# Two cross attentions of a decoder: projections in pairs, maxima earlier

## The reference

```python
# first block: 16 heads of 8
qc = _heads(x @ Wcq + bcq)
kc = _heads(cross_input @ Wck + bck)
vc = _heads(cross_input @ Wcv + bcv)
attc = jnp.einsum('bhqd,bhkd->bhqk', qc, kc) * scale
y = y + jnp.einsum('bhqk,bhkd->bhqd', jax.nn.softmax(attc, axis=-1), vc)
...
# second block, _mha of x over the normed context: 16 heads of 32
q = jnp.einsum('bsc,hcd->bhsd', xn, wq)
k = jnp.einsum('btc,hcd->bhtd', yn, wk)
v = jnp.einsum('btc,hcd->bhtd', yn, wv)
a = jax.nn.softmax(jnp.einsum('bhsd,bhtd->bhst', q, k) * D ** (-0.5), axis=-1)
o = jnp.einsum('bhst,bhtd->bhsd', a, v)
```

## Time and profile before

| what | us |
|---|---|
| median of 3 runs | 2286.98 |
| lowest, highest | 2262.93, 2294.28 |
| the profiled execution | 2294.59 |
| its span, first to last instruction | 2292.4 |
| busy in it: TensorE | 1837.0 (80%) |
| VectorE, ScalarE, GpSimd | 1177.9, 969.5, 524.5 |
| first cross attention, first to last shift matmul | 323.1 |
| last cross attention, first query product to its output projection | 602 (1478.2 to 2080.3) |

### The profile page before, as it was taken

How to read it: one execution, slowest core, us unless ns; L and a number is a source line. 1 busy time by engine, 2 the same in 40 slices (tenths; PEclk the granted TensorE clock), 3 DMA queues, 4 the chain that set the end, 5 groups by cost and what they waited for, 6 DMA issues and landing times. The chain is left out here.

```text
span 2292.4 us, 42946 instructions
## 1 busy us (share of the span) xinstructions
PE 1837.0 (80%) x16607; PEld 1007.5 (44%) x16607; DVE 1177.9 (51%) x2374; ACT 969.5 (42%) x1576; POOL 524.5 (23%) x392
## 2 busy tenths in 40 slices
PE   2774584999998339989899498579999999997598
PEld 1452361232233316654466265324445445454365
DVE  2664487777773335448642466434555555541322
ACT  1442262777776222211354244214554554553133
POOL 2112312000000000006544000024445445442000
PEclk8896696788887659999999779759999999998699
DMA  8414322211110221000000000021121121100010
GB/s 221 126 52 127 88 67 47 44 43 43 32 29 1 97 56 42 28 14 1 1 1 1 1 2 16 5 54 37 41 51 38 41 51 36 42 23 1 19 37 28
DMA packets 111896, 96.47 MB, mean 42 GB/s; under 512 B 21696, under 2 KB 97128, under 8 KB 111208
## 3 DMA queue, kind: packets, MB, share of 16 engines
q1 hardware_dynamic: 111720, 94.04, 15.7%
HBM read 51.30 MB, written 19.86 MB: 31 GB/s over the span
## 5 line engine op out<-in xcount | busy, mean ns | idle before, releaser
L2102 DVE TENSOR_REDUCE ta_mxp<-ps 128x1 f32<-128x401 f32 x512 | 267.2, 570 | 275.9 <-PE ps L2021 275.8
L1154 DVE TENSOR_REDUCE ac_mxp<-ps 128x2 f32<-128x802 f32 x256 | 244.7, 991 | 91.6 <-PE ps L1070 90.2
L2125 ACT ACTIVATE ta_prob<-ps 128x2048 f32<-128x2048 f32 (+1 forms) x112 | 196.5, 1755 | 146.9 <-PE ps L2057 146.9
L1183 ACT ACTIVATE cT<-ps 128x512 f32<-128x512 f32 (+1 forms) x416 | 225.7, 595 | 62.9 <-PE ps L1095 54.9
L1109 PE MATMUL ps<-cT 128*32 128x256 f32 (+1 forms) x1664 | 157.5, 456 | 0.5 <-ACT cT L1183 0.5
L2021 PE MATMUL ps<-ta_kb,ta_qb 96*128 96x401 bf16 x512 | 138.6, 355 | 16.4 <-DMA ta_kb<-ta_kh 12.2
L2053 PE MATMUL ps<-qxf,ta_k 32*128 32x256 f32 (+1 forms) x1664 | 133.6, 405 | 12.8 <-ACT ta_shiftT L2143 9.2
L2565 PE MATMUL ps<-xT,e_wi 128*128 128x512 f32 x256 | 116.1, 613 | 15.0 <-DMA e_wd<-in_e_down 10.2
L1070 PE MATMUL ps<-ac_kb,ac_qz 50*128 50x401 bf16 x512 | 100.7, 401 | 25.2 <-DMA ac_qb<-qc 18.5
L2575 PEld LDWEIGHTS ps<-e_wd,e_hid 128*128 128x128 f32 x1024 | 116.9, 192 | 7.6 <-issue 7.6
L2188 POOL TENSOR_TENSOR yT<-ta_prob 128x1024 f32<-128x1024 f32 x40 | 94.0, 2350 | 110.1 <-ACT ta_prob L2125 93.6
(11 more groups left out here) (323 smaller groups left out, 3507.0 us busy)
## 6 DMA issues: line engine op xcount, KB each, us to landing
ta_kb<-ta_kh SPq DMA_DIRECT2D x128, 100.1 KB
ac_kb<-kc SPq DMA_DIRECT2D x192, 50.0 KB
ta_kb<-ta_kl SPq DMA_DIRECT2D x64, 100.1 KB
v<-p_vt SPq DMA_DIRECT2D x16, 256.0 KB, 3.2
a_vs<-v SPq DMA_DIRECT2D x32, 128.0 KB, 2.7
e_wi<-in_e_in SPq DMA_DIRECT2D x8, 512.0 KB, 3.5
e_wd<-in_e_down SPq DMA_DIRECT2D x16, 256.0 KB, 3.6
kc<-c_part SPq DMA_DIRECT2D x12, 300.0 KB, 3.0
```

The costliest lines, as they stand in the source:

```text
L1154: v.tensor_reduce(mxp[:, qt * G + 2 * gg:qt * G + 2 * gg + 2, c:c + 1], k.ps[:, i % 2 * 2:i % 2 * 2 + 2, 0:401], AX.X, ALU.max).then_inc(s ...
L1183: a.activation(prob[0:rows, n % 3, h, :], k.ps[0:rows, bank(("part", n, h)), :], ACT.Exp, scale=scale).then_inc(exp_done.s, 1)
L2102: v.tensor_reduce(mxp[:, qt * G + g, c:c + 1], k.ps[:, turns.bank(slot), 0:401], AX.X, ALU.max).then_inc(scores_read.s, 1)
L2125: a.activation(prob[0:rows, n % 3, :, 0:w], k.ps[0:rows, 2:6, 0:w], ACT.Exp, scale=scale).then_inc(exp_done.s, 1)
```

## The change

In `stage_long` the count of plain products runs six key tiles ahead instead of three (EARLY), with a cap for the first tiles, and none but the first group's are issued ahead of the first shift. In the last cross attention groups s and s + 1 (s even) now belong to two batches that lie on the two halves of the partitions; their key chunks, and their value tiles, are issued next to each other (in even groups the keys of the next two, in odd ones the values of the next two). `Turns` gives a step three lists: three maxima; the other maxima, between values and row sums; projections after the row sums. `weigh` is split into `values` and `ones`. `stage_queries` is gone: the stage makes the queries itself after three key pairs, keeps their bf16 halves for a while in two buffers of the exponents, stores them to memory on SP, and loads a group's from there. Key and value buffers go from three to four and from two to three. The first negation is a scalar_tensor_tensor (−2 m + m) instead of a tensor_scalar.

```diff
-    NS, G, KT, NBUF, SLOTS, EARLY = BH // 4, 4, KT_CTX, 4, 16, 3
+    NS, G, KT, NBUF, SLOTS, EARLY = BH // 4, 4, KT_CTX, 4, 16, 6
...
-        return min(NS * SLOTS, SLOTS + (n + EARLY) * SLOTS // KT)
+        return min(NS * SLOTS, SLOTS + min((n + EARLY) * SLOTS // KT, 3 * (n + 1) // 2 + 1))
...
-                for i in range(SLOTS, issued(-1) if issued(-1) > SLOTS else SLOTS):
-                    plain_scores(i)
                 shift_rows(0)
-                done = max(SLOTS, issued(-1))
+                done = SLOTS
...
-                if 0 <= s + 2 < groups and p < 4:
-                    late.append(("key", s + 2, p))
-                if 0 <= s + 1 < groups and 2 <= p < 6:
-                    late.append(("value", s + 1, p - 2))
-                if 0 <= s + 1 < groups and p == STEPS - 1:
-                    late.append(("shift", s + 1, 0))
+                if s % 2 == 0 and s + 2 < groups and p < 4:
+                    late += [("key", s + 2, p), ("key", s + 3, p)]
+                if s == -2 and p >= 3:
+                    late += [("value", 0, p - 3), ("value", 1, p - 3)]
+                if s % 2 == 1 and 0 < s + 1 < groups and p < 4:
+                    late += [("value", s + 1, p), ("value", s + 2, p)]
                 m = [("max", s + 1, n) for n in range(*MAX_AT[p])] if 0 <= s + 1 < groups else []
                 early, m = m[0:3], m[3:]
-                mixed = []
-                for a, b in itertools.zip_longest(late, m):
-                    mixed += [x for x in (a, b) if x is not None]
-                for when, some in ((0, early), (1, mixed)):
+                if 0 <= s + 1 < groups and p == STEPS - 1:
+                    m.append(("shift", s + 1, 0))
+                for when, some in ((0, early), (1, m), (2, late)):
...
-MAX_AT = ((0, 6), (6, 12), (12, 17), (17, 22), (22, 27), (27, 32), (32, 32))
+MAX_AT = ((0, 5), (5, 10), (10, 15), (15, 20), (20, 26), (26, 32), (32, 32))
...
-def stage_queries(nc, k, srcT, w, full, high, low):
...
-def stage_cross(nc, k, name, scale, cT, wk, wv, q, qh, ql, both, out):
+def stage_cross(nc, k, name, scale, cT, wk, wv, srcT, wq, q, qh, ql, both, out):
...
+    def batch(s):
+        return s // 8 + 2 * (s % 2)
+
+    def part(s):
+        return s // 2 % 4
+
     def half(s):
-        return slice(64 * (s // 8), 64 * (s // 8) + 64)
+        return slice(64 * (s % 2), 64 * (s % 2) + 64)
 
     def at_batch(s):
-        return (s // 4) % 2 * W
+        return s // 8 * W
...
-        k32 = sb("k32", [P, 3, T_CTX])
+        k32 = sb("k32", [P, 4, T_CTX])
...
-        vs = sb("vs", [P, 2, KT_CTX, P])
+        vs = sb("vs", [P, 3, KT_CTX, P])
...
+        high_q, low_q = (prob[:, n, :, :].rearrange("p g c -> p (g c)").bitcast(BF16).rearrange("p (j c) -> p j c", j=4)
+                         for n in range(2))
+        units = [(j, c) for j in range(4) for c in range(2)]
...
+                    if kind in ("key", "value") and s % 2 == 1:
+                        return
                     free(slot)
                     bank = k.ps[:, turns.bank(slot), :]
-                    j = s % 4
+                    if kind in ("key", "value"):
+                        free((kind, s + 1, n))
+                        banks = (bank, k.ps[:, turns.bank((kind, s + 1, n)), :])
+                        j = part(s)
...
-                        pe.matmul(bank[:, 0:w], wk[half(s), j * P:(j + 1) * P],
-                                  cT[half(s), at_batch(s) + t0:at_batch(s) + t0 + w],
-                                  start=True, stop=True).then_inc(made.s, 1)
+                        for r in (s, s + 1):
+                            pe.matmul(banks[r % 2][:, 0:w], wk[half(r), j * P:(j + 1) * P],
+                                      cT[half(r), at_batch(r) + t0:at_batch(r) + t0 + w],
+                                      start=True, stop=True).then_inc(made.s, 1)
                     elif kind == "value":
-                        for t in range(4 * n, min(4 * n + 4, KT_CTX)):
-                            rows, c0 = tile_rows(t), at_batch(s) + t * P
-                            ins = pe.matmul(bank[0:rows, (t % 4) * P:(t % 4 + 1) * P], cT[half(s), c0:c0 + rows],
-                                            wv[half(s), j * P:(j + 1) * P], start=True, stop=True)
-                        ins.then_inc(made.s, 1)
+                        last = min(4 * n + 4, KT_CTX) - 1
+                        for t in range(4 * n, last + 1):
+                            for r in (s, s + 1):
+                                rows, c0 = tile_rows(t), at_batch(r) + t * P
+                                ins = pe.matmul(banks[r % 2][0:rows, (t % 4) * P:(t % 4 + 1) * P], cT[half(r), c0:c0 + rows],
+                                                wv[half(r), j * P:(j + 1) * P], start=True, stop=True)
+                                if t == last:
+                                    ins.then_inc(made.s, 1)
...
-                def weigh(s, p):
+                def values(s, p):
...
-                        for ones in (False,) if p in ADDED else (False, True):
+                        for g in range(G):
+                            ins = pe.matmul(k.ps[32 * g:32 * g + 32, 6, 0:N], vs[0:rows, s % 3, t, 32 * g:32 * g + 32],
+                                            prob[0:rows, n % 3, g, (t % 2) * N:(t % 2 + 1) * N],
+                                            start=(t == 0), stop=(t == KT_CTX - 1), skip_group_check=True)
+                    if p in ADDED and p - 1 not in ADDED:
+                        ins.then_inc(probs_used.s, 1)
+
+                def ones(s, p):
+                    n = s * STEPS + p
+                    if p in ADDED and p - 1 not in ADDED:
+                        return
+                    if p not in ADDED:
+                        for t in tiles_of(p):
+                            rows = tile_rows(t)
                             for g in range(G):
-                                w = k.ones[0:rows, 0:32] if ones else vs[0:rows, s % 2, t, 32 * g:32 * g + 32]
-                                o = k.ps[32 * g:32 * g + 32, 6, N * ones:N * ones + N]
-                                ins = pe.matmul(o, w, prob[0:rows, n % 3, g, (t % 2) * N:(t % 2 + 1) * N],
-                                                start=(t == 0 and not ones), stop=(t == KT_CTX - 1), skip_group_check=True)
+                                ins = pe.matmul(k.ps[32 * g:32 * g + 32, 6, N:2 * N], k.ones[0:rows, 0:32],
+                                                prob[0:rows, n % 3, g, (t % 2) * N:(t % 2 + 1) * N],
+                                                start=False, stop=(t == KT_CTX - 1), skip_group_check=True)
                     if p - 1 in ADDED:
...
+                def queries():
+                    for u, (j, c) in enumerate(units):
+                        if u > 3:
+                            pe.wait_ge(copied.s, copied.at(u - 3))
+                        pe.matmul(k.ps[:, 2 + u % 4, :], wq[:, j * P:(j + 1) * P], srcT[:, c * 512:(c + 1) * 512],
+                                  start=True, stop=True).then_inc(asked.s, 1)
...
                         for slot in turns.slots[s, p, 0]:
                             ring(slot)
-                        if s * STEPS + p > 0:
-                            weigh(*divmod(s * STEPS + p - 1, STEPS))
+                        if n > 0:
+                            values(*divmod(n - 1, STEPS))
                         for slot in turns.slots[s, p, 1]:
                             ring(slot)
-                weigh(NS - 1, STEPS - 1)
+                        if n > 0:
+                            ones(*divmod(n - 1, STEPS))
+                        for slot in turns.slots[s, p, 2]:
+                            ring(slot)
+                        if (s, p) == (-2, 2):
+                            queries()
+                values(NS - 1, STEPS - 1)
+                ones(NS - 1, STEPS - 1)
...
+                for u, (j, c) in enumerate(units):
+                    cols = slice(c * 512, (c + 1) * 512)
+                    v.wait_ge(copied.s, copied.at(u + 1))
+                    v.tensor_copy(high_q[:, j, cols], q[:, j, cols]).then_inc(parted.s, 1)
+                    v.wait_ge(parted.s, parted.at(2 * u + 1))
+                    v.tensor_tensor(low_q[:, j, cols], q[:, j, cols], high_q[:, j, cols], ALU.subtract).then_inc(parted.s, 1)
...
-                    v.tensor_scalar(high, mx[:, :], -1.0, None, ALU.mult).then_inc(vec.s, 1)
+                    v.scalar_tensor_tensor(out=high, in0=mx[:, :], scalar=-2.0, in1=mx[:, :],
+                                           op0=ALU.mult, op1=ALU.add).then_inc(vec.s, 1)
...
+                    if n == 0:
+                        a.wait_ge(stored.s, stored.at(128))
...
-                        for slot in turns.slots[s, p, 1]:
+                        for slot in turns.slots[s, p, 1] + turns.slots[s, p, 2]:
                             if slot[0] != "max":
                                 take(slot)
```

(52 more changed lines are left out.)

51 lines of the change are left out of this document (15 added, 36 removed).

## The result

The changed kernel takes 2194.43 us (median, 2190.82 to 2199.52) against 2290.63 us for the kernel before: a ratio of 0.966, interval 0.961 to 0.972. The kernel before spreads from 2258.17 to 2308.81 us over all its runs here, and a ratio with an interval leaves the slowest of its set out, so that it isn't the quotient of the medians (0.958 here) and doesn't compare with the ratio of another set. The forecast was 2187 with 2163 to 2212 as its own range. By the two profiled executions 2292.4 us became 2191.1, 101.3 less where the sum had 107.7.

What follows compares the result with a forecast made beforehand. Bounds: in the first cross attention TensorE's wait on negated maxima and the clock fall behind it, in the last TensorE's own order. 2294.6 − 54 − 48 − 5.7 = 2187 us, own range 2163 to 2212.

Steps and rivals of the forecast that it cites:

- First cross attention, −54: First cross attention, maxima six tiles ahead: fifteen periods from 21.54 to 17.9 us, −54 us, between −13 and −68.
- The wait's own price: First cross attention: removing TensorE's wait on the negated maxima saves 0.9 us a period at full clock, between 0.86 and 1.54.
- Two small terms: First cross attention: a clock fall in the tail, worth 3.6 us, set against one fall that may remain.
- The rival of a clock that goes on falling: First cross attention: the wait only changes its owner, the clock keeps falling, −13 us remains, 2228 us; chance 0.13.
- Last cross attention, −48: Last cross attention: paired projections overlap, net 3.2 us a group, period 31.2 us, −48 us over fifteen groups.
- the wait for the bank: Last cross attention, step 1: the pair waits for the ring bank holding the fourth maximum, about 0.55 us once a group.
- The order inside a step (values, maxima, sums, projections) moves no further work: Last cross attention: reordering values, maxima, sums and projections within a step changes no other work; no term in the sum.
- The negation, nothing: Last cross attention, negation before the shift: replacing the tensor_scalar gives 0.2 us at most, nothing in the sum.
- The beginning, −5.7: Last cross attention's start, first product to first scores: −5.7 us, between +2 and −9.
- Late keys: Last cross attention: every second group's keys have no slack; 3 us late each gives 2208 us, included in the 0.76 forecast.
- A lost clock in the last stage: Last cross attention: new holes make TensorE lose full clock; one fall a group gives 2241 to 2262 us; chance 0.06.
- No overlap: Last cross attention: two row halves don't run side by side, the stage keeps about 2 us, 2239 us; chance 0.05.

Runs made afterwards that it cites:

- the filled wait: Kernel before, wait on the negated maxima kept, TensorE multiplying 24 dummy 128 x 128 products meanwhile: 2258.91 us, ratio 0.9965 to the kernel before.
- maxima moved: Changed kernel, last cross attention's maxima spread 5, 4, 5, 5, 9, 4, 0 over the steps, those beyond a step's sixth behind its row sums: 2197.50 us.
- the old negation: Changed kernel with the last cross attention's negation as a tensor_scalar on 8 columns again: 2199.73 us, one run.
- maxima and queries together: Changed kernel with the maxima spread 5, 4, 5, 5, 9, 4, 0 and the first queries' transfers ahead of the keys': 2194.45 us, 0.957 of the kernel before.
- the joined order: Changed kernel with each step's row-sum products directly behind its value products, later maxima behind them: 2220.23 us, ratio 0.973 to the kernel before.
- the run on one half: Changed kernel with both members of each projection pair read from the same 64 rows: 2244.71 us, ratio 0.983 to the kernel before.

## Why the prediction was right, and where it was off

**First cross attention, −54: right**, −54.1 with the tail. The wait's own price, taken as 0.9 between 0.86 and 1.54, measured 0.90; the steady period, predicted 17.9, is 17.79; the rest was the clock, as the filled wait shows. Two small terms were set against each other and came out otherwise, so that the last half us of the agreement is luck: one low period remained, but it is the first (20.30 us at 0.75), and the tail gave 1.1 instead of 3.6. One reading was off: of the eleven low periods before, the first has no such wait ahead of it, its low clock comes from the stage before; ten periods, and the tail, had the fall behind the wait. And the size hangs on the execution that was profiled, with its ten falls: against the lowest time of the kernel before, 2258.17 us, the whole change is worth 64 us and not 101.

The rival of a clock that goes on falling is out. The rule that stood behind it, in the Trainium skill's "TensorE: Matmul & The Clock Gate", section "Why this matters for your kernels", puts such drops down to idle gaps longer than this wait. The profile before doesn't agree: eleven of its fifteen waits of 1.54 us had a fall right behind them, and with the wait filled none came. Nor was the wait the only cause: with it gone, three of the traces (maxima moved, the old negation, maxima and queries together) still have one period at 0.91, of 19.2 us, in this stage:

```profile
594.55:613.71 19.16, 18.20 (x200) 6.13 (x198) 15.60 (x20) 16.24 (x31) 1.32 (x3) 0.91 0.20 44
```

TensorE's idle times ahead of that fall, 0.45 and 0.37 us (until 597.67 and 599.59), stand in the next period too (616.84 and 618.76), which kept 1.00. Its cause stays open.

**Last cross attention, −48: 7 us too much.** A group gained 2.66 instead of 3.2 us. By its terms: the pairs 3.54 (3.5 predicted, overlap complete as bet); the wait for the bank 0.62 (0.55), in the step named; the maxima 0.63 (0.3), as before the change they also waited 0.31 us a group (4.0 us over thirteen, 2.4 of it for ScalarE's copies, second table by line). The step that failed is the sentence "The order inside a step (values, maxima, sums, projections) moves no further work". A block of value products takes 0.89 us where row sums follow it (1726.45 to 1727.34) and 1.00 where maxima do (1710.26 to 1711.26); a row-sum product takes 0.54 in the one place and 0.65 in the other (1716.83 to 1717.48). Over a group that is 0.9 us, and the joined order gave it back. 0.9 less the 0.33 that the maxima gained more is the miss of half a us a group.

**The negation, nothing: right in the sum, wrong in its reason.** The form changes nothing, but the step isn't covered. The new order puts the shift ahead of the last row sums, so TensorE waits 0.82 us for it instead of 0.23; as much comes back, since the row sums now hide the copy of the shift (0.58 before, 0.14 after). What the prediction missed is who sets that wait: GpSimd. It held back 0.48 us a group in the changed kernel and 1.2 with the maxima moved (31.70 to 30.50).

**The beginning, −5.7: 3 us too little by the table, half of it a matter of the cut.** The order was as predicted, queries' transfers last (11.16 us of waiting, until ta_qb), and the first maximum comes 34.0 instead of 37.2 us after the first product. The sum counts the table load and the block's change, 1.6 us, behind the first product; they lie ahead of it (the idle time there grew from 1.55 to 3.08 us), and the table has them in the row above. The other half is a price: the twelve issues of queries take 5.64 us, not 7.5. Before, when the queries came out of the core's own memory (SBUF), an issue of theirs took as long as one of keys, 5.03 us for eight:

```profile
1492.17 5.03 SPq L2209 DMA_DIRECT2D ta_qb<-qxh  x8
```

Now they come from the DRAM outside the core, and eight take 3.83. The sum carried the old price over; that the new source is what makes them shorter no run isolates.

**Late keys** did not come: no maximum waits for a transfer after the first group. The prediction was right that there is hardly any slack: the last key issue ahead of the first maximum at 1704.48 ends at 1702.71, 1.77 us before it, as long as such a transfer took to land before the change (1507.67 to 1509.44). **A lost clock in the last stage** did not come either: 1.00 with a hole of 0.82 and one of 0.59 us in each group. **No overlap** would have been 2245 rather than 2239 us, as the run on one half shows.

## What to carry to other kernels

Price a short wait of TensorE by what the clock does behind it: in the profiled execution 11.6 us of waiting cost 41.4 us more in clock, and useless products in the hole bought those back. Look at the clock of the other executions too, as one of the same kernel seems to have paid little of it. Here products that followed others of their own kind were cheaper than the same products with something between, 0.9 us a group, so an edit that only reorders can have a price too. And where a tiny VectorE instruction takes several times its shortest duration, look at what GpSimd ends at the same moment: here moving that one instruction was worth 0.48 to 1.2 us a group, and spreading the work before it alone 0.04 (31.74 to 31.70).

## What the hardware showed beyond that

VectorE and GpSimd hold each other up. The negation of 128 x 8 elements takes 0.18 to 0.20 us alone and 0.67, 0.80 or 1.64 beside GpSimd's addition, ending 0.04 to 0.05 us after it, in both forms; the reduction ahead of it, with its one input, takes 0.19 us while the addition runs (1706.72). The same stands at the stage's beginning, where a cast of the queries takes 0.42 us alone and 1.74 (from 1443.32) beside GpSimd's split of the keys (1442.89 to 1448.14), and a subtraction 0.69 and 3.59 (from 1445.09). The other way round is seen once: GpSimd's cast of the keys at 1442.89, begun while such a subtraction (from 1442.71) was running, takes 1.89 us, and 1.51 to 1.52 in the other fifteen groups. The Trainium skill says this in "SBUF — State Buffer", section "Who interferes with whom": a VectorE instruction with two inputs in SBUF contends with a GpSimd instruction that reads SBUF, and one in a mode that uses two ports contends with GpSimd too; whichever is issued first keeps the shared ports for its whole instruction and the other is blocked; a reduction never contends. The cases above agree; that the tensor_scalar and the cast ran in such a mode no trace here shows. The prediction gave 0.2 us for that instruction without asking what its 0.80 was made of.
